# Feed-forward stage of a graph network kernel: chunks of 2, 2, 4, 8, 8, 8, 8, 4, 2, 2 and 1 node tiles for six of 8 and one of 1, and its inputs loaded during the attention stage

## The chip, the cores and the metric

The kernel runs on one core of one Trainium2 chip. The metric is the device time of one execution in microseconds (us). The engines are TensorE (PE in the profile, with its weight loads as PEld), VectorE (DVE), ScalarE (ACT), GpSimd (POOL) and SyncE (SP, which here only issues DMAs). Each has its own instruction stream, and semaphores order them against each other.

## The reference, cut to what matters

There are 6250 nodes of 256 values (49 tiles of 128 nodes, the last with 106) and 200,000 edges. A relational graph layer comes first, then attention over the edges, then the part that this change is about:

```
attn_out = out.reshape(n, DIM) @ Wp + bp            # out: sum of weighted V over the edges of a node
h1 = layer_norm(h + attn_out, ln1_g, ln1_b)
ffn_out = gelu(h1 @ W1 + b1, approximate=False) @ W2 + b2      # 256 -> 1024 -> 256
y = layer_norm(h1 + ffn_out, ln2_g, ln2_b)
x = _layernorm(h + y)
```

Everything is float32.

## The kernel before

The program is a row of stages. At the end of each, every engine passes `meet`, which waits until all five have come. The last two stages matter here.

**Attention** walks 1664 columns of 128 edges in 416 quads of four. GpSimd gathers K and V rows of a quad into one of 12 slots of a ring (`rows`) in the big buffer `big`; TensorE spreads the queries and, eight quads later (`LAG_B`), scatters the weighted V rows of the quad into the sums of their nodes (L1389), two groups a quad, each counted in `x_sum`. A slot is free when its quad has been scattered. SyncE loads small tables for it (`x_tables`, L1340 and L1342) and has nothing left to do some 50 us before the stage ends.

**Feed-forward** works on chunks of node tiles in steps: `chunks` has six chunks of 8 tiles and one of 1. In step n

- VectorE does the first normalisation of chunk n-1 (L1674 to L1676), then the second normalisation of chunk n-3, the sum with x1 and its statistics (L1736, L1667), then the final scaling of chunk n-4 (L1738) and the division by the attention denominators of chunk n (L1711 to L1716). It adds the output of the network for the first group of chunk n-2 (L1700, L1704), adds the projection and x1 for chunk n (L1724, L1728), adds the network's output of the other group, and ends with `roots(n)`: the variances of all three kinds go together through one square root on ScalarE (L1686, L1840, L1689, L1691).
- TensorE does, for each group of up to 4 tiles of chunk n-2, the transposes of h1 (L1757) and the first product (L1771: 8 slices of the 1024, through two PSUM banks that ScalarE empties with GELU, L1825). Then come the second product of the first group (L1780), the projection of chunk n tile by tile (transposes L1757, products L1792), and the second product of the other group.
- ScalarE copies the transposes to SBUF (L1818 for h1, L1835 for the projection), computes GELU and the square root. It works in order: the copies for the next step stand behind the square root of this one, and that root waits for `roots(n)` on VectorE.

So a chunk takes five steps from its projection to its output. The stage has 11 steps, and TensorE works on the network in steps 2 to 8.

SyncE loads in this stage, from its start, Wp, six vectors, x1 of tiles 0 to 7, W1, b1, W2 and then the rest of x1 (`f_io`, L1636 to L1646). ScalarE and TensorE wait for weights before their first instruction (`s_fw`, `s_fw0`). The weights and the buffers of the stage lie in `edge_s`, the end of `big`, which the ring of the attention stage also covers.

Of the kernel before, what the change touches and what calls it, by code (L numbers as in the profile page):

```python
# [34 lines left out]
P = 128  # L35
N, D, E = 6250, 256, 200000
# [3 lines left out]
FC = FFN // P  # L40
KC = D // P
LOG_P = 7
W = -(-N // P)
# [15 lines left out]
QUAD = 4  # L59
# [3 lines left out]
QUADS = WALK // QUAD  # L63
# [5 lines left out]
CHQ = CH // QUAD  # L69
ROW_RING = 3 * CHQ  # L70
ROW = 2 * D + HEADS
LAG_B = 2 * CHQ
SPAN = CH + 1
LEADS = 3
PENS = 3 * P + 4
assert CH * CHUNKS == WALK and CHUNKS <= P
DST, SRC, WGT, REC = 0, 1, 2, 4
LOW = -1e30
EPS = 1e-5
# [55 lines left out]
def build(nc, a, out):  # L135
    ctx = ExitStack()
    with ctx:
        def sb(name, cols, dt=F32, rows=P):
            return ctx.enter_context(nc.sbuf_tensor(name, [rows, cols], dt))

        def sem(name):
            return ctx.enter_context(nc.semaphore(name))

        def dram(name, shape, dt=F32):
            return nc.dram_tensor(name, shape, dt, kind="Internal").ap()
# [3 lines left out]
        x1_store = dram("x1_store", (NP_, D))  # L149
# [9 lines left out]
        big = sb("big", W * D + EDGE_S)  # L159
        node_b, edge_s = big[:, 0:W * D], big[:, W * D:]  # L160

        walk_s = sb("walk_s", 4 * WALK)
# [31 lines left out]
        cut = Cut(early)  # L194
# [3 lines left out]
        cut = Cut(node_a)  # L198
# [8 lines left out]
        cut = Cut(edge_s)  # L207
# [10 lines left out]
        cut = Cut(node_b)  # L218
# [20 lines left out]
        cut = Cut(walk_s)  # L239
# [11 lines left out]
        cut = Cut(node_a)  # L251
# [3 lines left out]
        cut = Cut(walk_s)  # L255
# [4 lines left out]
        cut = Cut(edge_s)  # L260
# [4 lines left out]
        cut = Cut(node_b)  # L265
        recs = cut(WALK_G * P * REC).rearrange("p (g e f) -> p g e f", g=WALK_G, e=P)
        pen_out = cut(WALK_G * PENS, BF16).rearrange("p (g n) -> p g n", g=WALK_G)
        cut = Cut(edge_s)
# [11 lines left out]

        rows = big[:, 0:ROW_RING * QUAD * ROW].rearrange("p (s k n) -> p s k n", s=ROW_RING, k=QUAD)
        cut = Cut(big[:, ROW_RING * QUAD * ROW:])
        parts = cut(2 * QUAD * HEADS).rearrange("p (s n) -> p s n", s=2)
        picked, spans = cut(2 * CH).rearrange("p (s c) -> p s c", s=2), cut(2 * CH)
        far = cut(2)
        cut = Cut(early)
# [4 lines left out]
        hot_t = sb("hot_t", 2 * QUAD * P)[:].rearrange("p (s n) -> p s n", s=2)  # L291
# [7 lines left out]
        sel_h, sel_c = sb("sel_h", HEADS), sb("sel_c", 2 * SPAN)[:].rearrange("p (s c) -> p s c", s=2)  # L299
        sel_t = sb("sel_t", P, rows=HEADS)  # L300

        cut = Cut(edge_s)
        wp = cut(KC * D).rearrange("p (k n) -> p k n", k=KC)
        w1 = cut(KC * FFN).rearrange("p (k n) -> p k n", k=KC)
        w2 = cut(FC * D).rearrange("p (k n) -> p k n", k=FC)
        vec = {n: cut(D) for n in ("bp", "ln1_g", "ln1_b", "ln2_g", "ln2_b", "b2")}
        b1c = cut(FC)
        att_t = cut(2 * D).rearrange("p (s k n) -> p s k n", s=2, k=KC)
        h1_t = cut(2 * KC * 512).rearrange("p (s k n) -> p s k n", s=2, k=KC)
        hid = [r.rearrange("p (k n) -> p k n", k=FC) for r in (cut(FC * 512), walk_s[:, 0:FC * 512])]  # L310
        CHUNK = 8
        recip = sb("recip", CHUNK * HEADS)
        roots_s = sb("roots_s", 2 * 3 * CHUNK)
# [47 lines left out]
        def node_rows(w):  # L361
            return min(N - w * P, P)
# [680 lines left out]
        s_xall = [sem(f"s_xall{k}") for k in range(-(-W // CHUNK))]  # L1043
# [5 lines left out]
        x1 = node_b[:].rearrange("p (w d) -> p w d", w=W)  # L1049
        chunks = [list(range(w, min(w + CHUNK, W))) for w in range(0, W, CHUNK)]  # L1050
# [259 lines left out]
        phase(sync=walk_io, gpsimd=walk_gather, vector=walk_vector, tensor=walk_tensor, scalar=walk_scalar)  # L1310


        s_kv = [sem(f"s_kv{k}") for k in range(ROW_RING)]
        x_spread, x_off, x_hot_t, x_q, x_mul, x_red, x_score = (Count(sem("s_x_" + n)) for n in (
            "spread", "off", "hot_t", "q", "mul", "red", "score"))
# [5 lines left out]
        x_hot, x_msg, x_sum, x_add = (Count(sem("s_x_" + n)) for n in ("hot", "msg", "sum", "add"))  # L1321
# [3 lines left out]
        ps_grow = pb[:, 7, 2 * P + 80:2 * P + 80 + HEADS]  # L1325
        SLOTS = QUADS + LAG_B + 1

        def chunk_at(n, lag):

            g, r = divmod(n - lag, CHQ)  # L1330
            return g if r == 0 and 0 <= g < CHUNKS else None

        def at_quad(n):
            return n if 0 <= n < QUADS else None

        def x_tables(e):
            for g in range(CHUNKS):
                x_below.free(e, g, 2)
                for h in range(HEADS):
                    e.dma_start(pens[h::HEADS, g % 2, :], pen_table[g * CH:(g + 1) * CH, :]).then_inc(x_tab[g % 2], 16)  # L1340
                x_chain.free(e, g, 2)
                e.dma_start(carries[:, g % 2, :], carry_table[g:g + 1, :].to_broadcast([HEADS, 4 * SPAN]))\  # L1342
                    .then_inc(x_tab[g % 2], 16)

        def tables_in(e, g):
            e.wait_ge(x_tab[g % 2], 16 * (HEADS + 1) * (g // 2 + 1))
# [10 lines left out]
        def x_tensor(e):  # L1357
# [20 lines left out]
            def scatter(q):  # L1378
                x_hot.done(e, q)
                x_msg.done(e, q)  # L1380
                if q % CHQ == 0:
                    x_weight.done(e, q // CHQ)
                for j in range(2):
                    x_add.free(e, 2 * q + j, 2)
                    if j == 1 and q % CHQ == CHQ - 1 and q < QUADS - 1:
                        x_weight.done(e, q // CHQ + 1)
                    for k in range(2):
                        i = 2 * j + k
                        ins = e.matmul(pb[:, 5 + j, 0:AW], hot_e[:, q % 2, i * P:(i + 1) * P],  # L1389
                                       rows[:, q % ROW_RING, i, D:ROW], start=(k == 0), stop=(k == 1))  # L1390
                    ins.then_inc(x_sum.sem, 1)

            spread(0)
            for n in range(SLOTS):
# [22 lines left out]
                if g is not None:  # L1417
# [6 lines left out]
                    e.transpose(ps_back, expo[:, 0:P], ident[:]).then_inc(x_back.sem, 1)  # L1424
                if at_quad(n - LAG_B) is not None:
                    scatter(n - LAG_B)

        def x_scalar(e):
# [30 lines left out]
            for n in range(SLOTS):  # L1459
                g = chunk_at(n, LAG_B)  # L1460
                if g is not None:
                    x_back.done(e, g)
                    at = g * CHQ % ROW_RING
                    x_sum.free(e, 2 * (g * CHQ + CHQ) - 1, 2 * ROW_RING)
                    e.activation(rows[:, at:at + CHQ, :, 2 * D:ROW],
                                 ps_back.rearrange("p (s k h) -> p s k h", s=CHQ, k=QUAD), ACT.Copy)
# [3 lines left out]
                                 scale=lead_hot[:, g % LEADS:g % LEADS + 1]).then_inc(x_weight.sem, 1)  # L1470
                if at_quad(n + 1 - LAG_B) is not None:
                    hot_from(n + 1 - LAG_B)
                if at_quad(n + 1) is not None:
# [130 lines left out]
        phase(sync=x_tables, gpsimd=x_gather, scalar=x_scalar, tensor=x_tensor, vector=x_vector)  # L1604


        s_fw0, s_fw = sem("s_fw0"), sem("s_fw")
        s_fc, s_rooted, s_vars = sem("s_fc"), sem("s_rooted"), sem("s_vars")
        f_att, f_turn, f_turned, f_proj, f_z, f_h1, f_w1, f_gelu, f_w2, f_y, f_out = (
            Count(sem("s_f_" + n)) for n in ("att", "turn", "turned", "proj", "z", "h1", "w1", "gelu", "w2", "y",  # L1610
                                             "out"))
        s_store = sem("s_store")
        groups = [list(range(w, min(w + 4, W))) for w in range(0, W, 4)]


        STEPS = len(chunks) + 4

        def chunk(n):
            return chunks[n] if 0 <= n < len(chunks) else []

        def groups_of(n):
            return [g for g, ws in enumerate(groups) if ws[0] in chunk(n)]
# [2 lines left out]
        turns = {}  # L1625
        for n in range(STEPS):
            for key in [("h1", w) for w in chunk(n - 2)] + [("att", w) for w in chunk(n)]:
                turns[key] = len(turns)

        def f_io(e):  # L1630
            def load_x1(k):
                lo, hi = chunks[k][0], chunks[k][-1] + 1
                e.dma_start(x1[:, lo:hi, :], x1_store[lo * P:hi * P, :].rearrange("(w p) d -> p w d", p=P))\
                    .then_inc(s_xall[k], 16)

            e.dma_start(wp, a["L1_gnn_Wp"].rearrange("(k p) n -> p k n", p=P)).then_inc(s_fw0, 16)  # L1636
            for n in vec:
                e.dma_start(vec[n], a["L1_gnn_" + n].rearrange("(a d) -> a d", a=1).to_broadcast([P, D]))\
                    .then_inc(s_fw0, 16)
            load_x1(0)  # L1640
            e.dma_start(w1, a["L1_gnn_W1"].rearrange("(k p) n -> p k n", p=P)).then_inc(s_fw, 16)
            e.dma_start(b1c, a["L1_gnn_b1"].rearrange("(k p) -> p k", p=P), allow_slow_non_contiguous=True)\
                .then_inc(s_fw, 16)
            e.dma_start(w2, a["L1_gnn_W2"].rearrange("(k p) n -> p k n", p=P)).then_inc(s_fw, 16)
            for k in range(1, len(chunks)):
                load_x1(k)  # L1646
            for w in range(W):
                f_out.done(e, w)
                e.dma_start(out[w * P:w * P + node_rows(w), :], x1[0:node_rows(w), w, :]).then_inc(s_store, 16)
            e.wait_ge(s_store, 16 * W)  # L1650

        def f_vector(e):
# [4 lines left out]
            rs = roots_s[:].rearrange("p (v k i) -> p v k i", v=2, k=3)  # L1657
# [10 lines left out]
                        lambda w: e.bn_aggr(moments[k][:, w, :], slot(w)))  # L1668

            def scale_of(k, w):  # L1670
                return rs[:, 0, k, w % CHUNK:w % CHUNK + 1], rs[:, 1, k, w % CHUNK:w % CHUNK + 1]

            def norm(k, g, b):
                return (lambda w: e.tensor_scalar(z(w), z(w), *scale_of(k, w), ALU.mult, ALU.add),  # L1674
# [55 lines left out]

            for n in range(STEPS):
                if chunk(n - 1):
# [17 lines left out]
        def f_tensor(e):  # L1750
# [44 lines left out]

            for n in range(STEPS):
                net = groups_of(n - 2)
# [10 lines left out]
        def f_scalar(e):  # L1808
# [18 lines left out]

            for n in range(STEPS):
                for g in groups_of(n - 2):
# [63 lines left out]
```

## Time and profile before

| | us |
|---|---|
| median of 3 runs | 5541.96 (5532.95 to 5542.82) |
| the profiled execution's own time | 5530.44 |
| its span | 5528.7 |
| end of the attention stage, first load of the feed-forward stage | 4986.95 |
| first projection product | 5005.38 |
| first product of the network | 5049.55 |
| last product of the network begins, 3.72 long | 5503.79 |
| last instruction of VectorE ends | 5524.02 |

All times in the rows are microseconds from the start of the span. A product of 128x256 in float32 shows as records in PE of which two make one instruction of the program. A row of the timeline gives start, length, engine, line, operation, what is written and read, how many, and in brackets the idle time of the engine before it and who ended it.

### The profile page before, as it was taken

Reading aid. Unit: us, or ns where it says so; the run is one execution under the profiler, and the core shown is the slowest. Engines: PE = TensorE matmul, PEld = TensorE weight load, DVE = VectorE, ACT = ScalarE, POOL = GpSimd, SP = SyncE. Lnnn points to the kernel's source line nnn. Section 1 sums busy time; section 2 is a strip of 40 time slices with the busy share of each in tenths; the row PEclk is TensorE's granted clock in tenths of the full one; section 3 lists DMA queues with packets and bytes.
Section 4 is the critical chain, followed back from the end, with each engine's and each line's share of the span. In section 5 each row is a group of like instructions: output and inputs, shape, how many; then the busy total and the mean of one; then the engine's idle time right before and its main releaser. Section 6 shows DMA issues by size and latency. Waiting matters only on the chain. (4 is left out here: it accounts for less than half of the span.)

```text
span 5528.7 us, 88186 instructions
## 1 busy us (share of the span) xinstructions
PE 4347.1 (79%) x19043; PEld 2884.5 (52%) x19043; DVE 4702.8 (85%) x15281; ACT 3267.3 (59%) x8844; POOL 3199.8 (58%) x3363
## 2 busy tenths in 40 slices
PE   7998777777777777554758888888888888886997
PEld 3444344444444434333436666666666666664555
DVE  6888999999999998554369999999999999994564
ACT  2888777777777776001236666666666666662221
POOL 2004777777777777771057777777777777750000
PEclk9999999999999999777879999999999999998999
DMA  5433333333333333335357777777777777752000
GB/s 171 132 126 113 105 106 105 105 105 106 106 106 103 104 104 105 106 105 118 107 158 215 216 212 211 212 209 212 211 210 212 212 209 212 211 158 70 8 16 24
DMA packets 349147, 778.95 MB, mean 141 GB/s; under 512 B 76927, under 2 KB 179926, under 8 KB 348628
## 3 DMA queue, kind: packets, MB, share of 16 engines
q0 software_dynamic: 214080, 658.04, 41.7%
q1 hardware_dynamic: 129138, 111.40, 6.4%
q10 hardware_dynamic: 5410, 3.83, 0.2%
q8 instruction: 174, 2.85, 0.2%
q14 instruction: 345, 2.83, 0.2%
HBM read 691.39 MB, written 81.59 MB: 140 GB/s over the span
## 5 line engine op out<-in xcount | busy, mean ns | idle before, releaser
L1353 POOL DMA_INDIRECT big<-kv_table,walk_s x1664 | 1582.2, 951 | 580.9 <-issue 477.7
L692 POOL DMA_INDIRECT big<-xt_table,big x1616 | 1545.2, 956 | 533.6 <-issue 493.7
L701 ACT ACTIVATE walk_s<-walk_s,big 128x128 bf16<-128x128 bf16 x4704 | 1498.8, 390 | 417.5 <-DVE walk_s L966 394.1
L839 PE MATMUL pb<-big,walk_s 128*128 128x256 f32 x3232 | 1026.3, 413 | 236.0 <-issue 129.6
L1389 PE MATMUL pb<-big,early 128*128 128x264 f32 x3328 | 840.6, 396 | 103.5 <-issue 83.4
L1006 DVE TENSOR_TENSOR node_a<-node_a,pb 128x256 f32 x1616 | 662.1, 410 | 245.8 <-PE pb L839 236.2
L1373 PE MATMUL pb<-node_a,hot_t 128*128 x3328 | 822.6, 390 | 27.6 <-issue 23.3
L839 PEld LDWEIGHTS pb<-big,walk_s 128*128 128x128 f32 x3232 | 616.5, 206 | 374.2 <-issue 162.9
L766 PE MATMUL pb<-walk_s 128*128 128x384 bf16 x1568 | 530.1, 338 | 352.3 <-ACT walk_s L701 325.6
L1389 PEld LDWEIGHTS pb<-big,early 128*128 128x128 f32 x3328 | 602.0, 191 | 224.7 <-issue 116.5
L1373 PEld LDWEIGHTS pb<-node_a,hot_t 128*128 128x128 f32 x3328 | 605.4, 192 | 112.3 <-issue 45.8
L1446 ACT ACTIVATE early<-off_e,one_p 128x512 f32<-128x512 bf16 x416 | 300.3, 722 | 491.6 <-PE pb L1389 491.5
L766 PEld LDWEIGHTS pb<-walk_s 128*128 128x128 bf16 x1568 | 153.0, 98 | 821.8 <-ACT walk_s L701 770.2
L1493 DVE TENSOR_TENSOR big<-big,pb 128x1024 f32<-128x1024 f32 x416 | 504.1, 1212 | 33.9 <-DMA big<-kv_table,walk_s 26.2
L1441 ACT ACTIVATE off_e<-iota_q,walk_s 128x128 bf16<-128x128 f32 x1664 | 525.8, 388 | 0.2
L768 PE MATMUL pb<-walk_s 128*97 128x384 bf16 x1568 | 518.5, 331 | 0.0
L1521 DVE TENSOR_TENSOR big<-big,pb 128x1024 f32<-128x1024 f32 x416 | 501.9, 1206 | 7.9 <-PE pb L1389 6.5
L1499 DVE TENSOR_REDUCE big<-big 128x32 f32<-128x1024 f32 x416 | 504.3, 1212 | 0.0
L1030 DVE TENSOR_SCALAR walk_s<-early,big 128x128 f32<-128x128 int16 x1616 | 481.3, 298 | 6.9 <-ACT node_a L737 6.7
L966 DVE TENSOR_SCALAR walk_s<-early,big 128x225 bf16<-128x225 int16 x1568 | 463.6, 296 | 0.0
L965 DVE TENSOR_SCALAR walk_s<-early,big 128x128 bf16<-128x128 int16 x1568 | 422.1, 269 | 41.2 <-PE pb L768 39.2
L1535 DVE SCALAR_TENSOR_TENSOR node_a<-node_a,walk_s,pb 128x264 f32 x832 | 397.5, 478 | 7.4 <-PE pb L1389 6.9
(275 smaller groups left out, 5535.7 us busy)
## 6 DMA issues: line engine op xcount, KB each, us to landing
xt_table<-big SPq DMA_DIRECT2D x98, 512.0 KB, 2.9
big<-kv_table,walk_s POOLq DMA_INDIRECT x1664, 3.7
big<-xt_table,big POOLq DMA_INDIRECT x1616
pens<-pen_table SPq DMA_DIRECT2D x832, 12.1 KB
kv_table<-big SPq DMA_DIRECT2D x49, 256.0 KB, 2.0
x_store<-big SPq DMA_DIRECT2D x49, 128.0 KB, 2.0
big<-in_x POOLq DMA_DIRECT2D x48, 128.0 KB, 3.3
big<-in_x SPq DMA_DIRECT2D x6, 1024.0 KB, 11.4
```

Source lines behind the costliest of these rows:

```text
L692: e.indirect_dma_start(sum_rows[:, q % SUM_ROWS, k, :], None, xt_table, bass.IndirectOffsetOnAxis(ap=idx_all[:, i:i + 1], axis=0))\
L701: ins = e.activation(hot_v[:, t % SORT_HOTS, v, :], hot_q[:, t % SORT_HOTS, :], ACT.Copy, scale=byte[:, t:t + 1])
L766: e.matmul(pb[:, 0, 0:3 * P], hot_c[:, t % SORT_HOTS, 0:P], vals, start=(u == 0), stop=last, skip_group_check=True)
L768: ins = e.matmul(pb[0:COLS - P, 1, 0:3 * P], hot_c[:, t % SORT_HOTS, P:COLS], vals, start=(u == 0), stop=last, skip_group_check=True)
L839: e.matmul(pb[:, SUM_AT + i % SUM_BANKS, 0:D], sum_hot[:, i % SUM_HOTS, :], sum_rows[:, q % SUM_ROWS, k, :], start=True, stop=True).then_i ...
L1006: e.tensor_tensor(to, to, pb[:, SUM_AT + i % SUM_BANKS, 0:D], ALU.add).then_inc(added.sem, 1)
L1353: e.indirect_dma_start(rows[:, q % ROW_RING, k, 0:2 * D], None, kv_table, bass.IndirectOffsetOnAxis(ap=src_i[:, i:i + 1], axis=0))\
L1373: ins = e.matmul(pb[:, q % 2 * 2 + k // 2, k % 2 * D:(k % 2 + 1) * D], hot_t[:, q % 2, k * P:(k + 1) * P], acc_q[:, bass.ds(at[k // 2], D) ...
L1389: ins = e.matmul(pb[:, 5 + j, 0:AW], hot_e[:, q % 2, i * P:(i + 1) * P], rows[:, q % ROW_RING, i, D:ROW], start=(k == 0), stop=(k == 1))
L1441: ins = e.activation(off_e[:, k * P:(k + 1) * P], iota_q[:, 0:P], ACT.Abs, bias=dl_f[:, i:i + 1], scale=-1.0)
L1493: e.tensor_tensor(keys, keys, pb[:, q % 2 * 2:q % 2 * 2 + 2, :].rearrange("p b (k n) -> p b k n", k=2), ALU.mult).then_inc(x_mul.sem, 1)
L1499: e.tensor_reduce(parts[:, q % 2, :].rearrange("p (k h) -> p k h", h=HEADS), rows[:, q % ROW_RING, :, 0:D].rearrange("p k (h d) -> p k h d ...
```

## The change

The loads of the feed-forward stage move from its own first instructions to the end of `x_tables`, SyncE's part of the attention stage. The weights and buffers that are loaded move to the part of `big` behind 8 quad slots (`LOADED`), so that they touch only ring slots 8 to 11 and some spare room; SyncE waits until the last quads in these slots (up to 407 of 0 to 415) have been scattered, and then issues them. x1 lies in slots 0 to 6; each of its seven pieces waits for the last quad in the slots that it covers (408 to 414). The buffer of the projection's transposes goes to `hot_t`, one of the two `hid` buffers goes to the start of `edge_s`.

The chunks of the feed-forward stage become `f_chunks` of 2, 2, 4, 8, 8, 8, 8, 4, 2, 2 and 1 tiles. Groups are cut inside a chunk, so there are now groups of 2, and 15 steps. The code of a step is the same.

```
@@ x_tables, behind its loop
+            def rows_free(words):
+
+                last = (words - 1) // (QUAD * ROW)
+                x_sum.done(e, 2 * (QUADS - 1 - (QUADS - 1 - last) % ROW_RING) + 1)
+
+            x_sum.done(e, 2 * max(QUADS - 1 - (QUADS - 1 - k) % ROW_RING for k in range(LOADED, ROW_RING)) + 1)
+            e.dma_start(wp, a["L1_gnn_Wp"].rearrange("(k p) n -> p k n", p=P)).then_inc(s_fw0, 16)
...
+            for k in range(len(chunks)):
+                lo, hi = chunks[k][0], chunks[k][-1] + 1
+                rows_free(hi * D)
+                e.dma_start(x1[:, lo:hi, :], x1_store[lo * P:hi * P, :].rearrange("(w p) d -> p w d", p=P))\
+                    .then_inc(s_xall[k], 16)
@@ the buffers
-        cut = Cut(edge_s)
+        cut = Cut(big[:, LOADED * QUAD * ROW:])
...
-        att_t = cut(2 * D).rearrange("p (s k n) -> p s k n", s=2, k=KC)
+        att_t = hot_t.rearrange("p s n -> p (s n)")[:, 0:2 * D].rearrange("p (s k n) -> p s k n", s=2, k=KC)
+        hid = [r[:, 0:FC * 512].rearrange("p (k n) -> p k n", k=FC) for r in (edge_s, walk_s)]
@@ the chunks
-        groups = [list(range(w, min(w + 4, W))) for w in range(0, W, 4)]
-        STEPS = len(chunks) + 4
+        sizes = (2, 2, 4, 8, 8, 8, 8, 4, 2, 2, 1)
+        firsts = [sum(sizes[:n]) for n in range(len(sizes))]
...
+        f_chunks = [list(range(w, w + n)) for w, n in zip(firsts, sizes)]
+        groups = [ws[k:k + 4] for ws in f_chunks for k in range(0, len(ws), 4)]
+        STEPS = len(f_chunks) + 4
@@ f_io
-            e.dma_start(wp, a["L1_gnn_Wp"].rearrange("(k p) n -> p k n", p=P)).then_inc(s_fw0, 16)
...
-            load_x1(0)
...
-            for k in range(1, len(chunks)):
-                load_x1(k)
```

SyncE where the two stages meet, before. `pens` and `carries` are the attention's tables, the rest are this stage's loads.

```order
L1342 DMA carries<-carry_table 8x68 [waits s_c_chain]
L1636 DMA big<-in_L_gnn_Wp 128x2x256 [waits s_meet]
L1638 DMA big<-in_L_gnn_bp 128x256
...
L1633 DMA big<-x_store 128x8x256
L1641 DMA big<-in_L_gnn_W 128x2x1024
L1642 DMA big<-in_L_gnn_b 128x8x1
L1644 DMA big<-in_L_gnn_W 128x8x256
L1633 DMA big<-x_store 128x8x256 x5
L1633 DMA big<-x_store 128x256
L1649 DMA out<-big 128x256 [waits s_f_out] x48
```

The same place in the changed kernel:

```order
L1345 DMA carries<-carry_table 8x68 [waits s_c_chain]
L1354 DMA big<-in_L_gnn_Wp 128x2x256 [waits s_x_sum]
L1356 DMA big<-in_L_gnn_bp 128x256
...
L1358 DMA big<-in_L_gnn_W 128x2x1024
L1359 DMA big<-in_L_gnn_b 128x8x1
L1361 DMA big<-in_L_gnn_W 128x8x256
L1365 DMA big<-x_store 128x8x256 [waits s_x_sum] x6
L1365 DMA big<-x_store 128x256 [waits s_x_sum]
L1659 DMA out<-big 128x256 [waits s_f_out,s_meet]
```

The wait on `s_meet` now stands behind the loads, ahead of the first output.

TensorE at the end of the stage, before: the last chunk of eight (two groups), then the last tile. L1757 are transposes, L1771 and L1780 the two products of the network.

```order
L1757 MATMUL pb<-ident,node_a 128x128 x8
L1771 MATMUL pb<-big 128x512 x16
L1780 MATMUL pb<-big 128x256 x32
L1780 MATMUL pb<-big,walk_s 128x256 x32
L1757 MATMUL pb<-ident,node_a 128x128 x2
L1771 MATMUL pb<-big 128x128 x16
L1780 MATMUL pb<-big 128x256 x8
```

And in the changed kernel, where the same lines are L1768, L1782 and L1791, and L1803 is the projection: the last chunk of four, two of two, and the last tile.

```order
L1768 MATMUL pb<-ident,node_a 128x128 x8
L1782 MATMUL pb<-big 128x512 x16
L1791 MATMUL pb<-big,walk_s 128x256 x32
L1768 MATMUL pb<-ident,node_a 128x128 x4
L1803 MATMUL pb<-big,hot_t 128x256 x4
L1768 MATMUL pb<-ident,node_a 128x128 x4
L1782 MATMUL pb<-big 128x256 x16
L1791 MATMUL pb<-big 128x256 x16
L1768 MATMUL pb<-ident,node_a 128x128 x2
L1803 MATMUL pb<-big,hot_t 128x256 x2
L1768 MATMUL pb<-ident,node_a 128x128 x4
L1782 MATMUL pb<-big 128x256 x16
```

One step's products, which were two groups of four tiles, are here one group of four or of two.

## Rows read from the trace of the kernel before

**Rows 1.** Busy by stretch: us, PE, PEld, DVE, ACT, POOL, granted clock, DMA share, GB/s
```profile
4987.00:5005.00 18.00, 1.09 (x4) 0.71 (x4) 3.62 (x11) 0.05 (x1) 0.00 (x0) 0.56 0.88 260
5005.00:5049.00 44.00, 26.20 (x100) 18.63 (x100) 32.07 (x106) 8.42 (x22) 0.00 (x0) 0.75 0.35 112
...
5122.00:5132.00 10.00, 6.36 (x15) 3.15 (x14) 9.38 (x34) 3.51 (x7) 0.00 (x0) 0.68 0.00 1
```

**Rows 2.** Timeline of SyncE: the first load of the stage and the last six
```profile
4986.95 0.41 SPq L1636 DMA_DIRECT2D big<-in_L_gnn_Wp  x1
...
4997.88 16.76 SPq L1633 DMA_DIRECT2D big<-x_store  x6
```

**Rows 3.** Timeline of TensorE: the ninth scatter from the end of the attention
```profile
4952.27 2.01 PE L1389 MATMUL pb<-big,early 128*128 128x264 f32 x8
```

**Rows 4.** Timeline of all engines: steps 0 and 1 of the feed-forward
```profile
5004.95 0.66 ACT L1835 ACTIVATE big<-pb 128x256 f32<-128x256 f32 x2 [24.46 <-DMA big<-in_L_gnn_W]
...
5005.38 2.07 PE L1792 MATMUL pb<-big 128*128 128x256 f32 x4 [7.17 <-ACT big L1835]
...
5016.89 1.10 PE L1792 MATMUL pb<-big 128*128 128x256 f32 x4 [0.30 <-DVEq L1727]
...
5020.55 0.17 DVE L1686 TENSOR_SCALAR roots_s<-mv 128x8 f32<-128x8 f32 x1
5021.61 0.73 DVE L1674 TENSOR_SCALAR node_a<-node_a,roots_s 128x256 f32<-128x256 f32 x2
...
5030.60 2.77 DVE L1716 TENSOR_TENSOR node_a<-node_a,recip 128x256 f32<-128x256 f32 x8
...
5032.25 2.07 PE L1792 MATMUL pb<-big 128*128 128x256 f32 x4
```

**Rows 5.** The chain that ended last: start, us, what (steps 2, 6 and 7)
```profile
5049.55 15.71 PE pb L1771 x32
5067.55 14.00 PE pb L1771 x32
...
5092.43 3.72 PE pb L1780 x16
...
5107.46 6.92 PE pb L1780 x32
...
5118.34 3.73 PE pb L1780 x16
...
5127.22 16.61 PE pb L1771 x32
...
5406.97 3.72 PE pb L1780 x16
...
5412.52 6.92 PE pb L1780 x32
...
5490.00 3.73 PE pb L1780 x16
```

**Rows 6.** Timeline of all engines between steps 2 and 3
```profile
5124.56 0.37 DVE L1686 TENSOR_SCALAR roots_s<-mv 128x8 f32<-128x8 f32 x2
...
5125.66 1.09 PE L1757 MATMUL pb<-ident,node_a 128*128 128x128 f32 x4 [3.17 <-ACT big L1818]
```

**Rows 7.** Timeline of TensorE: the last tile, step 8
```profile
5497.23 6.10 PE L1771 MATMUL pb<-big 128*128 128x128 f32 x32 [3.30 <-ACT big L1818]
5503.79 3.72 PE L1780 MATMUL pb<-big 128*128 128x256 f32 x16 [0.46 <-ACT big L1825]
```

**Rows 8.** Timeline of VectorE: the end of the kernel
```profile
5511.66 2.67 DVE L1738 TENSOR_SCALAR big<-node_a,roots_s 128x256 f32<-128x256 f32 x8
...
5514.24 0.41 DVE L1700 TENSOR_TENSOR node_a<-node_a,pb 128x256 f32<-128x256 f32 x1
...
5519.88 2.67 DVE L1738 TENSOR_SCALAR big<-node_a,roots_s 128x256 f32<-128x256 f32 x8
...
5523.61 0.41 DVE L1738 TENSOR_SCALAR big<-node_a,roots_s 128x256 f32<-128x256 f32 x1
```

More of the change, by code:

```diff
@@ L71 @@
 ROW = 2 * D + HEADS
+LOADED = 2 * CHQ
 LAG_B = 2 * CHQ
@@ L76 @@
 assert CH * CHUNKS == WALK and CHUNKS <= P
+assert W * D + FC * 512 <= LOADED * QUAD * ROW
 DST, SRC, WGT, REC = 0, 1, 2, 4
@@ L307, in build @@
         b1c = cut(FC)
-        att_t = cut(2 * D).rearrange("p (s k n) -> p s k n", s=2, k=KC)
         h1_t = cut(2 * KC * 512).rearrange("p (s k n) -> p s k n", s=2, k=KC)
-        hid = [r.rearrange("p (k n) -> p k n", k=FC) for r in (cut(FC * 512), walk_s[:, 0:FC * 512])]
+        att_t = hot_t.rearrange("p s n -> p (s n)")[:, 0:2 * D].rearrange("p (s k n) -> p s k n", s=2, k=KC)
+        hid = [r[:, 0:FC * 512].rearrange("p (k n) -> p k n", k=FC) for r in (edge_s, walk_s)]
         CHUNK = 8
@@ L1310, in build @@
         phase(sync=walk_io, gpsimd=walk_gather, vector=walk_vector, tensor=walk_tensor, scalar=walk_scalar)
+        s_fw0, s_fw = sem("s_fw0"), sem("s_fw")
         s_kv = [sem(f"s_kv{k}") for k in range(ROW_RING)]
@@ L1343, in x_tables @@
                     .then_inc(x_tab[g % 2], 16)
+            def rows_free(words):
[3 more added lines that the diff above has]
+            e.dma_start(wp, a["L1_gnn_Wp"].rearrange("(k p) n -> p k n", p=P)).then_inc(s_fw0, 16)
+            for n in vec:
+                e.dma_start(vec[n], a["L1_gnn_" + n].rearrange("(a d) -> a d", a=1).to_broadcast([P, D]))\
+                    .then_inc(s_fw0, 16)
+            e.dma_start(w1, a["L1_gnn_W1"].rearrange("(k p) n -> p k n", p=P)).then_inc(s_fw, 16)
+            e.dma_start(b1c, a["L1_gnn_b1"].rearrange("(k p) -> p k", p=P), allow_slow_non_contiguous=True)\
+                .then_inc(s_fw, 16)
+            e.dma_start(w2, a["L1_gnn_W2"].rearrange("(k p) n -> p k n", p=P)).then_inc(s_fw, 16)
+            for k in range(len(chunks)):
[3 more added lines that the diff above has]
+                    .then_inc(s_xall[k], 16)
         def tables_in(e, g):
@@ L1604, in build @@
         phase(sync=x_tables, gpsimd=x_gather, scalar=x_scalar, tensor=x_tensor, vector=x_vector)
-        s_fw0, s_fw = sem("s_fw0"), sem("s_fw")
         s_fc, s_rooted, s_vars = sem("s_fc"), sem("s_rooted"), sem("s_vars")
@@ L1612, in build @@
         s_store = sem("s_store")
-        groups = [list(range(w, min(w + 4, W))) for w in range(0, W, 4)]
-        STEPS = len(chunks) + 4
+        sizes = (2, 2, 4, 8, 8, 8, 8, 4, 2, 2, 1)
+        firsts = [sum(sizes[:n]) for n in range(len(sizes))]
+        assert sum(sizes) == W and max(sizes) <= CHUNK
+        f_chunks = [list(range(w, w + n)) for w, n in zip(firsts, sizes)]
+        groups = [ws[k:k + 4] for ws in f_chunks for k in range(0, len(ws), 4)]
+        STEPS = len(f_chunks) + 4
         def chunk(n):
-            return chunks[n] if 0 <= n < len(chunks) else []
+            return f_chunks[n] if 0 <= n < len(f_chunks) else []
         def groups_of(n):
@@ L1630, in f_io @@
         def f_io(e):
[L1631 to L1634, printed above, removed]
-            e.dma_start(wp, a["L1_gnn_Wp"].rearrange("(k p) n -> p k n", p=P)).then_inc(s_fw0, 16)
-            for n in vec:
-                e.dma_start(vec[n], a["L1_gnn_" + n].rearrange("(a d) -> a d", a=1).to_broadcast([P, D]))\
-                    .then_inc(s_fw0, 16)
-            load_x1(0)
[L1641 to L1644, printed above, removed]
-            for k in range(1, len(chunks)):
-                load_x1(k)
             for w in range(W):
@@ L1670, in scale_of @@
             def scale_of(k, w):
-                return rs[:, 0, k, w % CHUNK:w % CHUNK + 1], rs[:, 1, k, w % CHUNK:w % CHUNK + 1]
+                at = next(w - ws[0] for ws in f_chunks if w in ws)
+                return rs[:, 0, k, at:at + 1], rs[:, 1, k, at:at + 1]
             def norm(k, g, b):
```

## The prediction

> **What bounds the kernel now.** I read the busy time by stretch first, then SyncE's timeline, the chain that ended last, and the timeline of all engines where that chain leaves TensorE. Only what lies behind 4986.95 changes, 537.1 us up to VectorE's last end at 5524.02. Three parts follow one another.
>
> - *Before the network, 62.6 us* (4986.95 to 5049.55). ScalarE's first copy stands until 5004.95 behind W2 [rows 4], while the DMAs move 260 GB/s [rows 1]. Then step 0 projects eight tiles, VectorE makes roots and normalises them, and step 1 projects eight more before TensorE sees the first h1.
> - *The network, 458.0 us* (5049.55 to 5507.51), bound by TensorE: a first product of four tiles is 14.00, a second 3.7 per tile [rows 5]. But between two steps the chain goes over VectorE and ScalarE. The last product of step 2 ends at 5122.07 (5118.34 + 3.73), VectorE's root starts at 5124.56, TensorE waits 3.17 for ScalarE's copies [rows 6], and the next first product starts at 5127.22: **a gap of 5.15**. That product takes 16.61 instead of 14.00 [rows 5]: in the ten microseconds around it the granted clock is 0.68 [rows 1], part at 1.2 GHz, so **2.6 more**. Over the six gaps of the stage (the first [rows 5], the last from 5493.73 to 5497.23, 3.50 for one tile [rows 5, 7]) the sum is 29.7, and the five late first products and the one at 5049.55 cost 12.8 together.
> - *The end, 16.5 us* (5507.51 to 5524.02). TensorE is done, and VectorE works off eight tiles' normalisation until 5511.66, two times eight scalings of 2.67, and the last tile [rows 8].
>
> **The loads.** They go from the path into the attention's last quads. The last quad that holds slots 8 to 11 is 407, the ninth scatter from the end, which ends at 4954.3 [rows 3], 32.7 ahead of the meeting. Before, all issues took 27.7 (4986.95 to 5014.64) [rows 2], so on SyncE they would end at 4982; the last piece of x1 must wait for the last scatter but one. SyncE then is at the meeting 2 to 4 before the others. ScalarE needs what landed in 18.0 before [rows 1, 4], so it is there in time; the gathers are issued by then and don't compete. Cover: the attention's last eight scatters. If it failed wholly the 18 would come back.
>
> **Before the network, after the change.** In step 1 of before, the first product stands 1.65 behind the start of the division (5030.60 to 5032.25, transposes and copies between) [rows 4]. Step 0: 0.85 of VectorE for the denominators of two tiles and those 1.65, 2.5. Two tiles' products at the slow clock: 2.07 [rows 4] and a little less, 3.8. From the last product (5017.99) to the root at 5020.55 it was 2.6 for eight tiles [rows 4]; for two tiles fewer operations stand in line, 2.2. Together 8.5. Step 1: root to normalisation 1.06 (5020.55 to 5021.61), normalisation and denominators 2.95 for two tiles, where eight take 9.0 (5021.61 to 5030.60) [rows 4], to the product 1.65, products 3.8, to the root 2.2: 11.7. From that root to a first product of two tiles 1.2 (the two transposes done ahead have only to be copied; four tiles need 2.66, 5124.56 to 5127.22 [rows 5, 6]). Sum **21.4, for 62.6: 41.2 gained**. Bounds: 19 if the clock stays at 2.4 GHz behind the attention, 24 if the short chains cost as much as those of eight tiles.
>
> **The network, after.** The products are the same, but there are 11 steps with 10 gaps for 7 with 6.
>
> - Projections: 45 tiles now lie here, 33 before. Eight take 11.3 (5096.15 to 5107.46), one takes 1.83 (5410.69 to 5412.52) [rows 5], so 1.83 + 1.36 for each further tile. Before: 4 x 11.3 + 1.83 = 47.1. After, with 4, 8, 8, 8, 8, 4, 2, 2, 1 tiles: 65.4. **+18.3**.
> - Pauses between the two groups of a chunk of eight: 2.29 (5065.26 to 5067.55) [rows 5], six before, four after: **-4.6**.
> - Gaps: a third set of roots adds 0.2 to the 5.15. Six lead to groups of four: 6 x 5.36. Three lead to two tiles: about 3.8 each, since 1.3 of transposes and copies falls away (between the 3.50 of one tile and the 5.15 of four); behind a projection of one tile 0.5 less. One to the last tile, 3.4. Sum 46.6, before 29.7: **+16.9**. Bounds for a short gap 3.3 and 5.4: 3 less, 5 more.
> - The slow clock behind each: ten, six at 2.2 and four (one of them behind the fill) at 2.5, which is the span between the rows' 1.71 and 2.61; 23.2 for 12.8, **+10.4**. A gap of 3.3 to 3.8 before two tiles isn't in the trace; the nearest, 3.50, is followed by a product bound by ScalarE, where the clock can't be read. I take the slow clock for all, as every gap of 5 shows it; the other end is none in the four short ones, 10 less.
> - A step with one group has no other product to put between the last GELU and the second product: TensorE waits 0.46 with one tile [rows 7], I take 0.6 with two, 0.8 with four (GELU is longer), six times: **+4.0**.
> - A first product of two tiles is 16 of 256 columns in place of half of 14.00; at the second product's rate 7.3: **+1.2** for four.
>
> VectorE's work ahead of the network's output must stay hidden. Worst is step 9: second normalisation of eight tiles (14 from 5497.23 to 5511.66 [rows 7, 8]), eight scalings 2.7, little else, about 19 against 20 until the second product's first tile; step 10 (four tiles, eight scalings) 13 against 14. Hidden, by one microsecond.
>
> Sum **+46.2**.
>
> **The end, after.** Behind the last product stand one tile's read, roots and second normalisation (5514.24 to 5519.88, 5.64), two scalings 0.7 in place of eight, roots 1.03 and the last scaling 0.41 [rows 8]: 7.8 for 16.5, **-8.7**.
>
> **Total: -41.2 + 46.2 - 8.7 = -3.7.** Nearly all that the loads and the short fill win is paid back at the four more gaps (27), with the twelve projections that only change place (18). Against the profiled 5530.4 that is 5526.7; the median of the runs stands 11.5 above that execution, so 5541.96 - 3.7 = **5538.3**.
>
> **The rivals.**
>
> - *The clock stays up in short gaps, faster.* Four late products lose 2.5 each less, the fill 2.5: 12.5 more, 5525.8, a gain of 0.3%. For it: within a chunk of eight the idle 2.29 leaves the next product at 14.00 [rows 5]. Against it: a gap of 3.17 idle is enough [rows 6]. Chance 0.15.
> - *The clock stays down through the short steps, slower.* From step 10 on TensorE works some 16 us at a time between gaps. If it stayed at 1.2 GHz over both steps of two tiles, their 29 us of products would take 12 more each: 5562. It decides where a step's work is over before the clock comes back. Against it: the first product of step 3 loses 2.6 of 16.61, so the clock was back some 5 us behind its start; and in the fill, in a stretch with gaps of 13 us and a mean clock of 0.75 [rows 1], the projection product came down from 2.07 to 1.10 within step 0 [rows 4]. Chance 0.06. The Trainium skill ("TensorE: Matmul & The Clock Gate", section "HAM oscillation — how this bites in real kernels") tells of a loop with short bursts of products between waits in which every burst began slow; taken whole it speaks for this rival and against the one before, and by it the time would be 5562 at the far end. The trace shows the slow start, not a slow burst.
> - *SyncE comes last to the meeting*, because the DMA queue pushes back on the late pieces of x1 (six took 16.76 [rows 2]), or the meeting waits for what has not landed: 3 to 8, 5544. Chance 0.07.
> - *The loads aren't hidden* and the change doesn't do what it says: 18 come back, 5556. It needs the queue at half its 260 GB/s. Chance 0.03.
>
> **How the numbers follow.** The forecast has 0.69, with its own range of 5528 to 5549: the bounds above give 13 less and 8 more, and the median moves by some 3. The range over all is 5525 to 5549, which leaves out the two slow rivals and the far ends. 0.2% is 11 us, about what a measurement of this kernel can tell from no change. Faster than that: the first rival and the forecast's lower edge, 0.21. Slower: the second and fourth rival and a small edge, 0.1. Within: 0.69.
>
> **What would show it.** The first projection product should stand within 4 us behind the attention's last scatter, the first product of the network 22 behind the meeting (before 62.6), the last product end 526 behind it (before 520.6), and the last scaling 8 behind that. Ten gaps of 3.3 to 5.4 should be seen, each with a slow first product. I am wrong if first products of two tiles take 7.3 and not 9.8, if the four steps at either end last longer than 18 to 29 us, or if VectorE is late for the network's output in steps 9 and 10.

## The result and the profile after

The changed kernel takes 5524.72 us in the median of 9 runs (5520.11 to 5530.01), the kernel before 5541.96 (9 runs, 5532.95 to 5548.76): a ratio of 0.9971, interval 0.9961 to 0.9981. That is 17 us faster, where 3.7 were forecast with "within 0.2%" as the likeliest outcome; the median lies 0.3 below the lower end of the stated range, and on the side that had 0.21.

The two profiled spans, 5528.7 and 5523.6, differ by 5.1 only. The last scatter of the attention begins at 4984.24 before and at 4994.15 after: the stages ahead happened to run 9.9 longer in that execution. The loads are not the cause: from the end of the scatter of quad 407, where they begin, to the end of the attention's last sum it is 32.6 in both traces. So every time below is counted from **the meeting**, the end of the attention's last sum on VectorE (4986.88 before, 4996.79 after). From there to the end of the span it was 541.8 before and is 526.8 after, **15.0 less**; the predicted working belongs against this number.

First the loads, in the timeline of the changed kernel (columns as in the rows above):

```profile
4964.22 0.41 SPq L1354 DMA_DIRECT2D big<-in_L_gnn_Wp  x1
...
4969.77 23.33 SPq L1365 DMA_DIRECT2D big<-x_store  x7
...
4996.30 0.49 DVE L1558 SCALAR_TENSOR_TENSOR node_a<-node_a,walk_s,pb 128x264 f32 x1 [0.40 <-PE pb L1412]
4997.04 0.10 DVE L1668 MEMSET roots_s<- 128x48 f32 x1 [0.25 <-POOLq L334]
...
4998.23 0.68 PE L1768 MATMUL pb<-ident,node_a 128*128 128x128 f32 x4 [2.07 <-DVE node_a L1727]
4998.76 0.66 ACT L1846 ACTIVATE hot_t<-pb 128x256 f32<-128x256 f32 x2 [8.37 <-PE pb L1768]
4999.20 3.58 PE L1803 MATMUL pb<-big,hot_t 128*128 128x256 f32 x8 [0.28 <-ACT hot_t L1846]
```

SyncE begins 32.6 ahead of the meeting and is done at 4993.10, 3.7 before it. Where ScalarE stood 24.46 behind W2 [rows 4], it now waits for TensorE's transposes and no longer for a load: the first projection product comes 2.4 behind the meeting, before 18.5.

The first products of the network in the chain that ended last (start, us, what), which answer to [rows 5]:

```profile
5016.63 8.59 PE pb L1782 x32
...
5042.49 8.88 PE pb L1782 x32
...
5075.83 16.54 PE pb L1782 x32
...
5124.69 15.71 PE pb L1782 x32
...
5281.06 16.32 PE pb L1782 x32
...
5459.99 8.77 PE pb L1782 x32
...
5481.72 7.25 PE pb L1782 x32
```

The fences that follow are timelines of TensorE and of VectorE at the end, which answer to [rows 7, 8].

```profile
5481.72 7.23 PE L1782 MATMUL pb<-big 128*128 128x256 f32 x32 [2.97 <-ACT big L1829]
5489.52 7.17 PE L1791 MATMUL pb<-big,walk_s 128*128 128x256 f32 x32 [0.56 <-ACT walk_s L1836]
...
5499.74 1.16 PE L1782 MATMUL pb<-big 128*128 128x128 f32 x8 [2.84 <-ACT big L1829]
5501.42 5.49 PE L1782 MATMUL pb<-big 128*128 128x128 f32 x24 [0.52 <-ACT big L1836]
5507.37 3.82 PE L1791 MATMUL pb<-big 128*128 128x256 f32 x16 [0.46 <-ACT big L1836]
```

```profile
5511.23 0.42 DVE L1711 TENSOR_TENSOR node_a<-node_a,pb 128x256 f32<-128x256 f32 x1 [6.65 <-PE pb L1791]
...
5516.87 0.73 DVE L1749 TENSOR_SCALAR big<-node_a,roots_s 128x256 f32<-128x256 f32 x2
...
5518.68 0.41 DVE L1749 TENSOR_SCALAR big<-node_a,roots_s 128x256 f32<-128x256 f32 x1
```

A first product of two tiles takes 7.25 at full speed. Three of the four are 1.3 to 1.6 late, the one at 5481.72, behind an idle of 2.97, is not late at all: over 5460 to 5469 the granted clock is 0.82, over 5481 to 5490 it is 1.00. The first product of the last tile, 6.10 before [rows 7], now takes 7.17 (from 5499.74 to 5506.91, in two rows), and the granted clock over 5499 to 5508 is 0.62.

### The profile page after: what moved, and what is told of

It reads as the page before. It is cut to its first block, busy times and chain, and to the rows that moved or that the text cites. A ratio compares the mean times of both kernels' runs of the same rounds, so it can differ in the third digit from the quotient of the medians.

```text
span 5523.6 us, 88413 instructions
## 1 busy us (share of the span) xinstructions
PE 4353.1 (79%) x19107; PEld 2903.1 (53%) x19107; DVE 4710.7 (85%) x15317; ACT 3282.0 (59%) x8872; POOL 3212.9 (58%) x3363
## 4 chain that ended last, share of the span: by engine, by line
PE 27%; DVE 14%; issue 9%; DVEq 2%; POOL 1%; ACT 1%; DMA 0%; POOLq 0%; ACTq 0%; SPq 0%
PE pb L1412 11%; DVE node_a L1558 4%; PE pb L1396 4%; PE pb L1782 3%; PE pb L1791 3%; DVE big L1516 2%; PE pb L1123 2%; DVE big L1544 1%; DVEq L325 1%; PE pb L1803 1%; PE pb L1129 1%; DVE peak L1583 1%; DVE peak L1585 1%; DVE top L1565 1%; PE pb L1447 1%
## 5 line engine op out<-in xcount | busy, mean ns | idle before, releaser
L1516 DVE TENSOR_TENSOR big<-big,pb 128x1024 f32<-128x1024 f32 x416 | 504.2, 1212 | 32.6 <-DMA big<-kv_table,walk_s 27.4
L1522 DVE TENSOR_REDUCE big<-big 128x32 f32<-128x1024 f32 x416 | 504.2, 1212 | 0.0
```

What stands on the lines that cost most here:

```text
L1516: e.tensor_tensor(keys, keys, pb[:, q % 2 * 2:q % 2 * 2 + 2, :].rearrange("p b (k n) -> p b k n", k=2), ALU.mult).then_inc(x_mul.sem, 1)
```

## The experiments

All were run against the kernel before on the same chip. On three of the four chips used for them the stages ahead take 1050 us longer and more (the changed kernel has 6574.67 on one of these); I did not look into why. Only e11 ran on a chip with times like those of the result. The stage from the meeting on does not differ: the changed kernel shows 527.0 on the slower chip and 526.8 in the result. This table is made from the timelines, in us from the meeting, one profile each; "network" runs from its first product to the end of its last, "end" from there to VectorE's last end, and 4.4 to 5.2 follow to the end of the span.

| kernel | first net product | network | end | whole stage | ratio to before (interval) |
|---|---|---|---|---|---|
| before | 62.7 | 458.0 | 16.5 | 541.8 | |
| the change | 19.8 | 494.6 | 7.9 | 526.8 | 0.9971 (0.9961 to 0.9981) |
| e0, the change again | 20.0 | 494.6 | 7.9 | 527.0 | 0.9985 (0.9971 to 0.9999) |
| e1, loads alone | 46.4 | 457.5 | 16.5 | 525.1 | 0.9975 (0.9964 to 0.9986) |
| e2, chunks alone | 37.2 | 494.7 | 7.9 | 544.3 | 0.9999 (0.9986 to 1.0012) |
| e3, loads, short front | 20.0 | 487.6 | 16.6 | 528.9 | 0.9981 (0.9970 to 0.9993) |
| e4, loads, short end | 46.3 | 464.0 | 7.9 | 522.7 | 0.9975 (0.9963 to 0.9987) |
| e7, the change with filler | 20.4 | 474.9 | 7.9 | 507.7 | 0.9954 (0.9937 to 0.9971) |
| e5, the change, copies ahead | 18.3 | 460.0 | 7.9 | 490.7 | 0.9924 (0.9905 to 0.9943) |
| e6, copies ahead, chunks of 8 | 43.8 | 430.1 | 15.7 | 494.2 | 0.9926 (0.9908 to 0.9944) |
| e8, copies ahead, short end | 43.7 | 437.4 | 7.9 | 493.5 | 0.9922 (0.9896 to 0.9949) |
| e9, copies ahead, 4 4 8 8 8 8 4 4 1 | 27.9 | 447.6 | 8.6 | 488.5 | 0.9900 (0.9874 to 0.9926) |
| e10, copies ahead, 4 8 8 8 8 8 4 1 | 33.7 | 436.5 | 8.5 | 483.3 | 0.9899 (0.9871 to 0.9926) |
| e11, copies ahead, 5 8 8 8 8 8 4 | 36.6 | 429.3 | 16.2 | 487.3 | 0.9894 (0.9878 to 0.9911) |

**Which part gains.** Four kernels take the change apart.

```
e1:  sizes = (8, 8, 8, 8, 8, 8, 1)                   in the changed kernel
e2:  the chunk part of the diff alone, in the kernel before
e3:  sizes = (2, 2, 4, 8, 8, 8, 8, 8, 1)             in the changed kernel
e4:  sizes = (8, 8, 8, 8, 8, 4, 2, 2, 1)             in the changed kernel
```

> The loads alone: the changed kernel with its chunks set back to six of 8 and one of 1. Measured from the meeting behind the attention to the end of the span the stage was 541.8 before and 526.7 with the change. Theory A (the chunks are worth nothing, the loads everything): the first projection product moves from 18.4 behind the meeting to about 2.5, the rest stays, so the stage is about 526 and the gain about 16, as large as the whole change's. Theory B (a good part of the gain is the short ends): the stage is about 532 and the gain 8 to 10.

> The chunks alone: the kernel before with the eleven chunks, its loads still at the start of the feed-forward stage. Theory A: the stage is 541 to 544 from the meeting, no different from before. Theory B: about 534, 8 less.

> Loads moved and only the front made short (2, 2, 4, five of 8, 1). From the terms that the changed kernel's trace shows: 27 less before the network, 27 more in it (12 projections, two more gaps with their slow starts, waits for the last GELU). Theory A: within 2 of the loads alone. Theory B: 6 less than the loads alone.

> Loads moved and only the end made short (five of 8, then 4, 2, 2, 1). The end behind TensorE is 8.6 shorter, two more gaps of 3.5, one slow start and three waits of 0.6 to 0.8 for the last GELU cost 9. Theory A: within 2 of the loads alone, the end behind the last product 8 long. Theory B: 6 less.

> The changed kernel again, as the yardstick for the other three of this job and for how much its times and its slow starts move from run to run. About 526.7 from the meeting; the granted clock behind each gap may fall otherwise: the late part of the ten first products was 16.7 together, 12 to 22 is expected here.

The loads alone give 525.1, 16.7 less than before and more than the whole change. The chunks alone give 544.3, 2.5 more than before and just outside the 541 to 544 of theory A, with a ratio of 0.9999. Against the loads alone the short front costs 3.7 and the short end gains 2.5, both together cost 1.7 to 1.9. So theory A holds for the whole, though neither half was as near to nothing as it said: 3.7 and 2.5 are outside the "within 2". The stage's start in e1, to be set beside [rows 4]:

```profile
6036.41 0.10 DVE L1668 MEMSET roots_s<- 128x48 f32 x1 [0.25 <-POOLq L334]
...
6037.36 2.77 DVE L1727 TENSOR_TENSOR node_a<-node_a,recip 128x256 f32<-128x256 f32 x8
```

e0 shows the same stage as the first profile to 0.2, and each of its first products is within 0.04 of the one in the first profile: which are late, and by how much, repeats. The timeline moves by much less than the medians, whose intervals of 0.1 to 0.15% to either side are 6 to 9 us. e1, e3 and e4 can't be told apart by their ratios, only by the timelines.

**The late first products.** Is it the clock?

```
+                    if first and i == min(2, len(ws) - 1):
+                        for _ in range(6):
+                            e.matmul(pb[:, 4, 0:D], ident[:], wp[:, 0, :], start=True, stop=True)
                     turn("h1", w)
```

> The changed kernel with six products of 128x256 on constant data, whose result nobody reads, ahead of the transposes that TensorE waits with between two steps (2.7 of the 3.2 to 3.4 that it idles). Nothing else waits for them. Theory clock: the late first products (16.7 together) are the clock that falls in the gaps, so most first products go back to 14.0 and 7.2 and the stage is 10 to 15 shorter. Rival: they are late for the GELU table load and ScalarE, then nothing changes or the stage gets longer by up to 3.

TensorE's timeline in e7, the first four-tile step (L1780 is the filler, L1787 the first product):

```profile
6118.47 2.75 PE L1780 MATMUL pb<-big,ident 128*128 128x256 f32 x12
6121.97 0.77 PE L1768 MATMUL pb<-ident,node_a 128*128 128x128 f32 x4 [0.75 <-ACT big L1834]
6123.22 14.00 PE L1787 MATMUL pb<-big 128*128 128x512 f32 x32 [0.47 <-ACT big L1834]
```

All first products are at 14.00 or 7.23, and that of the last tile falls from 7.17 to 5.18 (1.16, 0.52 and 3.50). The stage is 19.3 shorter than e0's, more than the 10 to 15 expected, and the granted clock over the network is 1.00, in the changed kernel 0.95. GELU's table load and ScalarE's order are the same, so the rival is out: the late part is the clock, which falls in the pauses between steps. Three pauses before four tiles are also 0.4 shorter, since their transposes take 0.77 or less and not 1.09 [rows 6]; the last two pauses are 0.1 and 0.2 longer.

**The gaps.** By the reading of [rows 6] their cause is ScalarE's order, and e5 tests it. There the copies of the next step's first group stand ahead of the square root:

```
+                for g in groups_of(n - 1)[:1]:
+                    copies(g)
                 if chunk(n) or chunk(n - 2) or chunk(n - 3):
                     e.wait_ge(s_vars, n + 1)
                     e.activation(roots_s[:, 0:3 * CHUNK], ...
```

> The changed kernel with ScalarE's order altered: the copies of the next step's first h1 group stand ahead of the square root, not behind it. Theory queue: the gaps (45 together) are ScalarE standing in the square root's wait with the copies behind it; then TensorE goes on after its transposes, gaps of 4 tiles fall from 5.2 to about 2.5, of 2 tiles to about 3 with the GELU wait, and the clock stays up. The stage is 30 to 38 shorter, about 492. Rival: TensorE would then wait for the first GELU, which is behind the root and two table switches, and only 10 or so is won.

> The same order of copies, with six chunks of 8 and one of 1 (loads moved). Theory: short chunks paid nothing because each gap costs 3.4 to 5.4 and a slow start; with cheap gaps they pay, so this one is 6 to 12 slower than the same order with the eleven chunks. Rival: the projections and the waits for the last GELU eat it as well, and the two are within 3.

TensorE in e5, one gap to four tiles and one to two (L1768 transposes, L1782 first product):

```profile
6103.16 0.60 PE L1768 MATMUL pb<-ident,node_a 128*128 128x128 f32 x4
6104.11 0.69 PE L1768 MATMUL pb<-ident,node_a 128*128 128x128 f32 x4 [0.34 <-ACT big L1827]
6105.27 14.13 PE L1782 MATMUL pb<-big 128*128 128x512 f32 x32 [0.47 <-ACT big L1827]
```

```profile
6073.03 1.99 PE L1782 MATMUL pb<-big 128*128 128x256 f32 x8 [0.53 <-ACT big L1827]
6077.14 7.13 PE L1782 MATMUL pb<-big 128*128 128x256 f32 x24 [2.12 <-ACT walk_s L1839]
...
6501.24 4.63 PE L1782 MATMUL pb<-big 128*128 128x128 f32 x24 [2.61 <-ACT big L1839]
```

36.3 less than the change, as the queue theory said. A gap to four tiles is now 1.9, before 5.0 to 5.4, with idle times of 0.34 and 0.47, and the clock stays up (1.00 over 6105 to 6120). Behind the first two slices of a two-tile product TensorE stands for the first GELU (2.12 here, 2.61 for the last tile), which waits for the root and the table load behind it. ScalarE at the first of these places (L1856 is the root, L1839 GELU):

```profile
6075.08 0.22 ACT L1856 ACTIVATE roots_s<-roots_s 128x24 f32<-128x24 f32 x1 [0.81 <-DVEq L1698]
6075.32 1.28 ACT L1839 ACT_TABLE_LOAD   x1
6076.62 0.84 ACT L1839 ACTIVATE walk_s<-pb,big 128x256 f32<-128x256 f32 x2
```

Behind that stand the clock fell once more: the 24 records took 7.13, in the two later steps of two tiles 5.45, and the granted clock over 6077 to 6084 is 0.76. The second part of e6's expectation fell: with cheap gaps the eleven chunks are 3.5 better than chunks of 8, not 6 to 12, nearer to the rival's "within 3". The order is worth 31 with chunks of 8 (525.1 to 494.2) too.

**Which chunks, once gaps are cheap.**

```
e9:   sizes = (4, 4, 8, 8, 8, 8, 4, 4, 1)    in e5
e10:  sizes = (4, 8, 8, 8, 8, 8, 4, 1)       in e5
e8:   sizes = (8, 8, 8, 8, 8, 4, 2, 2, 1)    in e5
e11:  sizes = (5, 8, 8, 8, 8, 8, 4)          in e5
```

> The altered order of copies with chunks of 4, 4, four of 8, 4, 4 and 1. With that order a gap before four tiles costs some 2.4, but the three groups of two tiles and the last tile still stand 1.0 to 2.6 within their first product, for the first GELU behind the root. Theory: groups of four escape this, because two slices of four tiles last longer than root and table load. Against the order with six chunks of 8 (494.2 from the meeting): 15 less before the network, 16 more in it, 6 to 7 less at the end, so about 488. Rival: the price of a step is not in the gaps but in projections and waits, then 494 or more.

> The same with chunks of 4, five of 8, 4 and 1: one step less at either end. Before the network the second projection of eight tiles costs 9 more than one of four, in the network 4 tiles and a gap fewer: about 489, within 2 of the one with 4 and 4.

> The altered order of copies with five chunks of 8, then 4, 2, 2 and 1: the front is not short. Against six of 8 with that order (494.2): the end 7.8 less, two more gaps and the stands in three short groups 6 more, so about 492. If short groups were free it would be 487.

> The altered order of copies with chunks of 5, five of 8, and 4: the last tile's own step is gone. Against 4, five of 8, 4 and 1 (483.3 from the meeting): one gap of 1.1 and a stand of 2.6 fewer, no projection tile moved ahead but one (1.4 more before the network, less in it), and behind TensorE four tiles' read, normalisation and scaling in place of one (12 to 13 for 8.5). Theory: 482 to 485, nothing won, because a step of one tile costs about what four tiles cost at the end. Rival: 3 or more won.

Four tiles at either end (e10) are the best stage, 483.3: 58.5 less than before. e10 was expected within 2 of e9 and beats it by 5. In e9 TensorE stands 2.50 for VectorE, which has the second normalisation of eight tiles and the scaling of eight others ahead of its read of the network's output, and goes on at a granted clock of 0.82 (these 32 records take 7.57 behind the same wait in e5):

```profile
6583.95 9.14 PE L1791 MATMUL pb<-big 128*128 128x256 f32 x32 [2.50 <-DVEq L1714]
```

That makes 4 of the 5. The same stand is 0.90 in e5 and in e8: the work of VectorE that the prediction held hidden by one microsecond shows once the gaps are short. In e10 the four-tile groups stand for nothing but their last GELU, and only the last tile pays the early one (3.07, and behind it 24 records in 5.49, 3.50 in e7):

```profile
6544.70 14.10 PE L1782 MATMUL pb<-big 128*128 128x512 f32 x32 [0.47 <-ACT big L1827]
6559.58 14.87 PE L1791 MATMUL pb<-big,walk_s 128*128 128x256 f32 x64 [0.78 <-ACT walk_s L1839]
6575.14 1.16 PE L1782 MATMUL pb<-big 128*128 128x128 f32 x8 [0.47 <-ACT big L1827]
6579.37 5.49 PE L1782 MATMUL pb<-big 128*128 128x128 f32 x24 [3.07 <-ACT big L1839]
```

e8 was expected at 492 and came at 493.5: short groups of two are not free. e11 came 2 above its expectation, at 487.3, and 4 above e10, so nothing is won by sparing the last tile its own step. e10's ratio is 0.9899; e9, e10 and e11 can't be told apart by their ratios. All of them beat both kernels clearly.

## Why the prediction was wrong about the size

Point by point, by the prediction's own steps; the forecast is the number before the arrow, what the trace shows stands behind it.

- **The loads: right.** SyncE at the meeting 2 to 4 early -> 3.7. Nothing came back: neither the rival "SyncE comes last" nor "the loads aren't hidden" happened. e1 puts a number of its own on this part, 16.7.
- **Before the network: 21.4 -> 19.8.** 1.6 too much, inside the stated bounds of 19 to 24. The products of two tiles at the slow clock make 0.9 of it: they were put at 3.8 twice, and took 3.58 in step 0 and 3.16 in step 1. The rest is 0.1 to 0.25 in each of the other terms, VectorE's normalisation with the denominators first (2.7 for 2.95).
- **The network: 504.2 -> 494.6.** This is where the forecast failed, and most of it is one term:
  - *The slow clock behind the gaps, 23.2 -> 16.7.* Two-tile products were taken as 2.5 late each, from the upper end of four-tile rows (1.71 to 2.61). They came 1.3, 1.6, 1.5 and 0.0 late. The six of four tiles cost 12.2 to my 13.2. The rows held a lower bound and I had named it (none in short gaps, "10 less"); the value should have been taken nearer the middle. The first rival, that the clock stays up in short gaps, came true in one step of these four, behind an idle of 2.97; the others stood behind 2.75 (the end of the fill), 3.41 and 3.21, so the one with the shortest idle was late.
  - *The last tile, which I took as unchanged:* 6.10 -> 7.17, 1.1 the other way. The 6.10 was read as bound by ScalarE; e7's 5.18 shows that it held slow clock too.
  - *The gaps, 46.6 -> 45.1* (3.84, 5.42, 5.03, 5.36, 5.36, 4.97, 4.96, 3.65, 3.41, 3.05). 1.1 of the 1.5 lies in three gaps to four tiles of about 5.0 and not 5.36, whose four transposes took 0.68 and not 1.09; the one to the last tile was 0.35 too dear.
  - *Projections, 65.4 -> 64.2.* One tile more costs 0.86 with two in a chunk, not 1.36: the first two share the transposes made ahead. And the 47.1 of before was 0.7 too low: two of its four projections of eight tiles took 11.66, not 11.3.
  - *Waits for the last GELU, 4.0 -> 3.8* (0.56 with two tiles, 0.78 with four); a first product of two tiles at full speed, 7.3 -> 7.25. Right.
  - These make 9.3 of the 9.6; the rest I can't place.
- **The end: 7.8 -> 7.9.** Right.
- **VectorE hidden in steps 9 and 10: right.** TensorE's second product runs through there without a wait for it, 14.87 and 7.17.
- **A sign that was stated wrongly.** The four steps of two tiles were to last 18 to 29, and lasted 25.9, 33.3, 21.7 and 18.0. The second holds a projection of eight tiles, and by the prediction's own terms (9.8 + 0.6 + 7.2 + 11.3 + 5.4) it should have been given 34.

Sum of the errors: 1.6 + 9.6, and 0.2 behind the last instruction, less 0.1 at the end, make the 11.3 between the forecast 3.7 and the 15.0 of the traces. The remaining 2 to the 17 of the medians is within their interval (10 to 22).

What stands of the argument is its mechanism. It said that the short chunks are paid back at the gaps, and that is what e2 shows: on their own they are worth nothing. But it put their price, against the loads alone, at 12 (12.3 = 46.2 - 8.7 - 25.2, where 25.2 is what of the front's 41.2 is not the 16 of the loads), and e1 and the change put it at 1.7. So the gain of the loads came through nearly whole; the step that failed is the price of the short chunks in the network, and in it the slow clock. The slower rival, a clock that stays down through the short steps, is refuted: over 5481 to 5490 the clock is 1.00, and ten of the eleven steps began slow (the last tile among them), but no second product of two tiles took more than its 7.17. The Trainium skill ("TensorE: Matmul & The Clock Gate", section "HAM oscillation — how this bites in real kernels") tells of a loop in which every burst of products behind a wait began slow. The trace agrees for these ten, and not for the one at 5481.72.

The base cost nothing. The profiled execution stood 11.5 below the median of before, but what was forecast is a difference, worked out behind 4986.95 alone and added to the median. Only when two spans are set against each other do the stages ahead come in, here with 9.9, and counting both from the meeting takes them out.

## What to carry to other kernels

Before chunks are cut finer to shorten the fill and the end of a pipeline, price the boundary between two chunks: here a gap of 3 to 5.4 without a product and up to 2.5 of slow clock behind it. Four more of them, with waits for the last GELU, and 12 projections that only change place (16 of the 37 by which the network is longer than in e1) ate a front that began 26 earlier and an end 9 shorter. Look first at what makes the boundary: an in-order engine that stands in a wait while work for the bottleneck, ready long before, is queued behind that wait. Moving two to four copies ahead of one square root was worth 31 to 36 us, twice what the whole change gained. Behind it the shape of the chunks brought up to 10.9 (from chunks of 8 to 4, five of 8, 4, 1), where the eleven chunks had lost 1.7 with the old order and won 3.5 with the new; the best shape was not run with the old order. And loads that wait for a whole stage to end can start when the part of the buffer that they overwrite is free.

## What the runs showed of the hardware that I had not expected

- The granted clock falls behind 3.0 of idle in some gaps and not in others. In the changed kernel an idle of 3.21 was followed by a first product of 8.76, one of 2.97 by 7.23, and one of 2.84 by a last tile whose 24 records took 5.49 for 3.50 at full speed. In e4 the same idle of 3.21 stands before both products of two tiles, and one took 8.65, the other 7.23. So the length of the idle alone does not decide it. Nor is it chance: the changed kernel, e0 and e2, three executions, two of them on slower chips, have the same products late by the same time, to 0.05. What does decide it can't be told from these runs.
- Products on constant data, whose result nobody reads, are worth their place: six of them in each pause, 2.75 long, take 19.3 off the stage, with the network at a granted clock of 1.00, that is at 2.4 GHz, for 0.95.
- The same program takes 5525 in the result and 6575 on the chip of e0, with a stage from the meeting on that agrees to 0.2 (526.8 and 527.0). The difference lies wholly ahead of the meeting.
